# Gated feed-forward with adapters and a top-2 router: gate rows later in the load queue, logits steps spread anew, early ranks one piece later

## What is computed

```python
def lora_add(base, inp, A, B):
    Ab = A[layer_idx][lora_indices]
    Bb = B[layer_idx][lora_indices]
    t = jnp.einsum('bri,bni->bnr', Ab, inp)
    return base + jnp.einsum('bor,bnr->bno', Bb, t) * SCALE
gate = lora_add(jnp.einsum('bnh,fh->bnf', x, W_gate), x, A_gate, B_gate)
up = lora_add(jnp.einsum('bnh,fh->bnf', x, W_up), x, A_up, B_up)
act = jax.nn.silu(gate) * up                       # F = 2752
down = lora_add(jnp.einsum('bnf,hf->bnh', act, W_down), act, A_down, B_down)
...
logits = x @ W_gate + b_gate                       # x is now down
_, top_idx = jax.lax.top_k(logits, TOP_K)
y_all = jax.nn.relu(jnp.einsum('bsd,edh->bseh', x, W_e) + b_e)
y = jnp.take_along_axis(y_all, top_idx[..., None], axis=2)
return y.mean(axis=2)
```

## Time and profile before

| what | value |
| --- | --- |
| median of 3 runs | 1908.52 us (1905.09 to 1914.23) |
| the profiled execution | 1906.02 us, its span 1904.2 us |
| PE busy | 1835.0 us (96%) |
| VectorE busy | 1205.3 us (63%) |
| GpSimd busy | 1082.8 us (57%) |
| ScalarE busy | 748.5 us (39%) |
| moved by DMA | 331.43 MB, 174 GB/s |
| mean granted clock of TensorE | 0.987 of full speed |

### The profile page before, as it was taken

One profiled execution on the slowest core, in us unless ns is written; L12 is line 12 of the kernel. 1 busy time (PEld: TensorE's weight loads), 2 busy tenths in 40 slices (PEclk: granted clock), 3 DMA queues, 4 the chain that ended last, 5 costly groups with the idle time before them and its releaser, 6 DMA issues.

```text
span 1904.2 us, 24886 instructions
## 1 busy us (share of the span) xinstructions
PE 1835.0 (96%) x8679; PEld 1529.2 (80%) x8679; DVE 1205.3 (63%) x1371; ACT 748.5 (39%) x1062; POOL 1082.8 (57%) x643
## 2 busy tenths in 40 slices
PE   7999999999998999999999999997979999999997
PEld 5788888888886878888888888886868888888885
DVE  8877888876466795767777666466787742244400
ACT  5544444444433335444444444433322333333332
POOL 2678898863434453545666444434434766666664
PEclk9999999999998999999999999998989999999998
DMA  5556566645566654443443435565724875676643
GB/s 205 168 207 227 204 210 235 228 135 180 190 209 208 210 193 139 138 135 123 152 168 130 159 111 197 196 230 171 243 86 154 239 191 143 170 188 188 155 93 53
DMA packets 118026, 331.43 MB, mean 174 GB/s; under 512 B 14081, under 2 KB 16001, under 8 KB 117633
## 3 DMA queue, kind: packets, MB, share of 16 engines
q1 hardware_dynamic: 99952, 268.06, 40.8%
q0 software_dynamic: 17952, 61.75, 13.4%
HBM read 248.62 MB, written 90.05 MB: 178 GB/s over the span
## 4 chain that ended last, share of the span: by engine, by line
PE 72%; POOL 8%; DVE 8%; issue 5%; DMA 5%; ACT 1%; SPq 1%; POOLq 0%; ACTq 0%; DVEq 0%
PE PS L1649 22%; PE PS L1650 21%; PE PS L1651 21%; DVE R L889 2%; DVE FT L1272 2%; DMA raw<-wt_scratch 2%; PE PS L1693 2%; PE PS L2000 2%; PE PS L1768 2%; DMA raw<-in_wp 1%; POOL brw L729 1%; POOL FT L672 1%; POOL FT L667 1%; POOL FT L664 1%; PE PS L1907 1%
## 5 line engine op out<-in xcount | busy, mean ns | idle before, releaser
L1649 PE MATMUL PS<-R,ring 128*128 128x512 f32 (+1 forms) x1800 | 708.5, 394 | 19.9 <-DVE R L920 9.4
L1650 PE MATMUL PS<-R,ring 128*128 128x512 f32 (+1 forms) x1800 | 703.2, 391 | 0.0
L1651 PE MATMUL PS<-R,ring 128*128 128x512 f32 (+1 forms) x1800 | 702.7, 390 | 0.0
L1649 PEld LDWEIGHTS PS<-R,ring 128*128 128x128 f32 x1800 | 339.4, 189 | 91.9 <-issue 16.7
L1651 PEld LDWEIGHTS PS<-R,ring 128*128 128x128 f32 x1800 | 338.9, 188 | 72.0
L1650 PEld LDWEIGHTS PS<-R,ring 128*128 128x128 f32 x1800 | 339.4, 189 | 65.6
L750 POOL TENSOR_TENSOR ring<-raw,ring 128x1024 fp32r<-128x1024 f32 x78 | 196.6, 2521 | 293.4 <-ACT ring L876 293.3
L1649 PE MATMUL PS<-ring,R 128*128 128x512 f32 x592 | 235.7, 398 | 17.7 <-DVE FT L1218 17.3
L729 POOL DMA_INDIRECT brw<-in_bgu,idx_b x88 | 92.8, 1055 | 262.4 <-DVE R L1041 216.8
L1650 PE MATMUL PS<-ring,R 128*128 128x512 f32 x592 | 234.2, 396 | 0.0
L1651 PE MATMUL PS<-ring,R 128*128 128x512 f32 x592 | 233.7, 395 | 0.0
(11 more groups left out here) (189 smaller groups left out, 2334.4 us busy)
## 6 DMA issues: line engine op xcount, KB each, us to landing
raw<-in_wp SPq DMA_DIRECT2D x124, 512.0 KB, 4.2
act_scratch<-FT SPq DMA_DIRECT2D x140, 256.0 KB, 4.8
FT<-act_scratch SPq DMA_DIRECT2D x70, 512.0 KB, 5.7
raw<-in_we SPq DMA_DIRECT2D x64, 512.0 KB, 6.0
raw<-wt_scratch SPq DMA_DIRECT2D x40, 512.0 KB, 6.6
out<-in_xn SPq DMA_DIRECT2D x17, 512.0 KB, 5.0
ytp<-in_wgb SPq DMA_DIRECT2D x32, 256.0 KB, 4.9
y_scratch<-FT SPq DMA_DIRECT2D x7, 1024.0 KB, 6.6
```

The lines of the kernel that those rows point to most:

```text
L1649: e.matmul(out_, hi, whi, start=start, stop=False, skip_group_check=True)
L1650: e.matmul(out_, hi, wlo, start=False, stop=False, skip_group_check=True)
L1651: return e.matmul(out_, lo, whi, start=False, stop=stop, skip_group_check=True)
```

## The change

Four things are altered.

- `load_wb` for s >= 2 gets the key of the step that frees its buffer plus 1.6 instead of plus 0.02; the first two are asked for a piece earlier.
- the steps 32 to 63 are spread over the pieces 26 to 35 as 2, 3, 3, 4, 4, 3, 3, 4, 4, 2 (before: over 26 to 34 as 2, 4, 4, 4, 4, 4, 3, 4, 3), and the sum and the choice move a piece back with the last of them;
- `early_ranks` stands behind piece 36 on PE, not behind piece 35, and `early_hots` moves back accordingly on VectorE;
- `early_table` stands between the third and the fourth remainder product of `last2`, not ahead of the first.

```diff
@@ -625,12 +625,12 @@
             if o < 32:
                 m = 10 + o // 2
             else:
-                m = 26 + sum(o - 32 >= n for n in (2, 6, 10, 14, 18, 22, 25, 29))
+                m = 26 + sum(o - 32 >= n for n in (2, 5, 8, 12, 16, 19, 22, 26, 30))
             return op_m(g, m) + 2.3 + 0.001 * o
 
         for g in range(NG):
             for s in range(16):
-                sp.add(l_key(g, 4 * max(s - 2, 0) + 3) - (4 if s < 2 else 0) + 0.02, load_wb, g, s)
+                sp.add(l_key(g, 4 * (s - 2) + 3) + 1.6 if s >= 2 else l_key(g, 0) - 4, load_wb, g, s)
@@ -1374,8 +1374,8 @@
-            dve.add(op_m(g, 34) + 2.38, l_sum, g)
-            dve.add(op_m(g, 34) + 2.39, choice, 2 * g)
+            dve.add(op_m(g, 35) + 2.38, l_sum, g)
+            dve.add(op_m(g, 35) + 2.39, choice, 2 * g)
@@ -1555,7 +1555,7 @@
-        dve.add(op_m(1, 35) + 0.5, early_hots)
+        dve.add(op_m(1, 36) + 2.31, early_hots)
         dve.add(op_m(1, 38) + 0.3, early_rows)
@@ -1873,6 +1873,8 @@
                     m = rem(g, 6, i)
                     if i < 2:
                         turn2(g, i)
+                    elif g and i == 2:
+                        early_table()
@@ -1965,10 +1967,8 @@
                         piece(g, s, kp)
-                        if g == NG - 1 and s == 6 and kp == 2:
+                        if g == NG - 1 and s == 6 and kp == 3:
                             early_ranks()
-                        if g == NG - 1 and s == 6 and kp == 4:
-                            early_table()
```

## The result

The changed kernel takes 1881.64 us (median of 4 runs, 1876.88 to 1882.01), the kernel before 1910.18 us (median of 4, 1905.09 to 1914.23): a ratio of 0.9846, 95% interval 0.9817 to 0.9876. That is 28.5 us less, where 31 were forecast, and inside the range. The profiled execution took 1882.01 us (span 1880.2).

What follows compares the result with a forecast made beforehand. PE was taken as the bound, busy 1835.0 of 1904.2 us. Gains 11.7 + 12.8 + 1.7 + 5.4 + 1.0 = 32.6, less about 1.6, gave 31 us: 1875.0 profiled, 1877.5 for a median, range 1867 to 1893.

Steps and rivals of the forecast that it cites:

- The ring (part 1): Stages 2 to 4, both halves: gate-row waits close a 15.9 us loop per two pieces; the change makes it 12.1.
- the price of its new place: SP's queue: the moved gate-row wait costs nothing, since the loads behind it wait for the same VectorE steps anyway.
- the second half's wave: PE's stalls and low clock in stages 2 to 4, second half: 13.8 us, of which 1.0 was left standing.
- stalls elsewhere: Some stage ends: about 1.6 us taken off the summed gain for small PE stalls that are now uncovered.
- the two waves: PE's stalls and low clock in stages 2 to 4: gains of 11.7 us, first half, and 12.8, second half.
- rival A: Stages 2 to 4: the load loop stays too long, 13.5 us a turn; 18 us gained, 1886 to 1893; chance 0.12.
- The steps (part 2): End of stage 5, both halves: the adds start at 1390.7, not 1393.9; bank waits of 1.7 us go.
- The ranks (part 3): Second half's early ranks: PE waits 3.5 us for the mask, not 8.7; gain of the place 5.4 us.
- what lies behind the ranks: Stage 6 adds, second half: about 1.8 us, as a new wait or low clock, in place of 2.0.
- 6.2 + 1.8: Forecast gains: 6.2 us from stage 5's end to the last product's tail, second half; 1.8 in first-half stages 5 and 6.
- The end of the first half (part 5): Adds of stage 6, first half: PE waits 0.5 to 2 us instead of 2.24; gain 1 us.
- The table (part 4): Second half's remainder products: same 12 matmuls; gathers keep some 5 us of slack; PE's own wait 0 to 0.5 us.

Runs made afterwards that it cites:

- the second pair of profiles: The kernel before and the changed kernel, both unchanged, profiled once more, one execution each: 1908.34 and 1879.88 us.

## Why the prediction was right, point by point

**The ring (part 1)** held in cause and size. The wait for the step ahead of the gate row was what made `a_lo` and the adds late; with it moved, SP's wait fell from 218.9 to 45.7 us, and the price of its new place was nothing, as put. Mis-sized was only the residue: I left 1.0 us of the second half's wave standing, since the bank wait at 1276.6 comes early, and took 1.6 us off the sum for stalls elsewhere. None is left: 91.96 us in both halves is what PE needs. So the two waves gave 27.5 us (25.7 in the second pair of profiles) for 24.5 forecast. The 12.1 us of the ring, which rival A took for too long, never showed, for PE is slower than that wherever there is adapter work and has enough in hand where there is none (10.9, then 12.8 us between gate rows).

**The steps (part 2)**: the wait for the adds of stage 5 went in both halves. **The ranks (part 3)**: a wait of 3.5 us was forecast, 3.38 measured. In the times of before (26.8 us later at the tail of stage 5) the adds of stage 5 start at 1390.6 and the mask is done at 1414.7, where 1390.7 and 1415.0 were forecast. That is luck in part. What ate the earlier start was not one more subtraction of GpSimd: the low part that took 3.35 us beside one at 1408.5 now takes 1.21, and in its place VectorE stands 1.92 us for ScalarE ahead of the low part of the down projection's adapter weights (L1051). The low part before:

```profile
1408.53 3.35 DVE L889 TENSOR_TENSOR R<-FT,R 128x1024 fp32r<-128x1024 f32 x1
```

and after:

```profile
1371.39 1.63 DVE L1051 TENSOR_TENSOR R<-brw,R 32x1024 fp32r<-32x1024 f32 x1 [1.92 <-ACT R L1046]
...
1378.84 1.21 DVE L889 TENSOR_TENSOR R<-FT,R 128x1024 fp32r<-128x1024 f32 x1
```

Mis-sized is what lies behind the ranks, forecast at 1.8 us as a wait or as low clock. It was low clock, for 6.8 us (1.0 of it before the ranks start) and not 3.4, and cost 2.5 us: from the ranks to the table 12.69 us, where the two other spreads, which kept their clock, took 11.73 with 1.5 of wait in it. The kernel with the 2.5 us delay met the 3.4 us of low clock that the forecast put, and took 11.73 as well. That and the first half's end make the difference between 6.2 + 1.8 and 5.5 + 1.2. **The end of the first half (part 5)** was forecast to wait 0.5 to 2 us and waits 2.17: the three steps more behind the adds of stage 5 cost as much as these adds gained, and I had taken too much of the gain. The gain of 1.2 us there is not in the second pair of profiles. The two other spreads, with two and four steps less behind these adds, have no wait at that place. **The table (part 4)** cost nothing, and its gathers' delay stayed covered.

**What the forecast lacked** was the clock in a stretch without stalls: I had counted it only behind waits. It took 4.5 us in the transposes in the first pair of profiles and 3.1 in the second. So the closeness of 31 forecast to 28.5 measured is luck in part: the waves gave 3.0 us more than their price and the transposes took more than that back. The profiled gain of 24.0 us in the first pair is smaller still by 1.9 us at the start and 3.6 in the expert part, which the second pair (28.5) doesn't show.

The rule of the Trainium skill on the port that VectorE shares with GpSimd ("SBUF — State Buffer", "Who interferes with whom") agrees with the changed kernel's trace: a step beside a subtraction still takes 2.87 us, alone 0.68.

```profile
1380.42 2.49 POOL L750 TENSOR_TENSOR ring<-raw,ring 128x1024 fp32r<-128x1024 f32 x1 [2.67 <-ACT ring L876]
...
1380.59 2.87 DVE L1272 CUSTOM_DVE_ANT_0 FT<-FT,ytp 128x512 f32<-128x512 f32 x1
1383.38 0.68 DVE L1272 CUSTOM_DVE_ANT_0 FT<-FT,ytp 128x512 f32<-128x512 f32 x1
```

Still, the price of the spread went in plain steps of 0.61 us and not in whole subtractions: in the changed kernel and in both other spreads exactly two steps of 2.87 or 2.88 us stand between the adds of stage 5 and the mask, so moving steps moved none of them.

## What to carry to other kernels

In an in-order load queue, a small load that waits for a consumer belongs behind the large loads whose own buffers are free at the same moment, not ahead of them: the wait itself can stay. Look for it where a queue's wait is long in total and an engine two steps down is idle for "DMA". Where one engine's list decides when a short result is ready, count the instructions between the last fixed point and that result. Here each was worth its plain duration, and the ones taken away all stood behind the last idle time of that engine, so no wait swallowed the gain.

## What was not expected of the hardware

The granted clock of TensorE fell from 2.4 to 1.2 GHz in a stretch of transposes and 8-column matmuls in which PE had next to no idle time, in some profiles early (13.9 to 14.4 us for the stretch), in others late or not (9.75 to 12.8 us), with the same instructions in it. With 2.5 us of extra matmuls 250 us ahead it stayed high in one execution, and with 3.4 us of them it fell in one. What it was, of what PE did in that stretch, that let the clock fall isn't settled by these runs, nor whether the moment or chance decides, and the fastest spread of steps met it too. One and the same kernel took 1865.94 us at a mean granted clock of 0.995 and 1874.69 at 0.990. A gain or loss of some 5 us between single executions of two variants of this kernel can therefore be the clock alone, and the row of its granted clock tells.
